# Hand-written unrolling of the inner loops, and a narrower wait in the linear attention, in a four-stage transformer kernel

## The reference

```python
# block 1: linear attention and a mixture of four dense experts (cut)
q_phi, k_phi = elu(q) + 1.0, elu(k) + 1.0           # 16 heads of 8
kv_prefix = cumsum(k_phi[..., :, None] * v[..., None, :], axis=1)
k_prefix = cumsum(k_phi, axis=1)
attn = einsum('bthd,bthdm->bthm', q_phi, kv_prefix) / (sum(q_phi * k_prefix, -1) + 1e-06)
x = x + sigmoid(delta @ w_gate.T + b_gate) * (attn @ w_o.T)
...
# block 2: mixture of 16 experts, fp4 weights; block 3: (x Wq^T) x^T x
# block 4: DEPTH = 6 layers, each
x = attn_layer(shift_tokens(x), Wqkv[i], ...) + x   # 16 heads of 64, windows of 32
x = ffn_layer(shift_tokens(x), ...) + x             # gated GELU, 341 hidden units
```

## Time and profile before

| what | value |
|---|---|
| median of 3 runs | 5524.06 us (5520.37 to 5528.53) |
| the profiled execution | 5523.19 us |
| its span, first to last instruction | 5521.5 us |
| mean granted TensorE clock | 0.937 of full speed |
| busy share of the span | TensorE 89%, VectorE 73%, ScalarE 69%, GpSimd 44% |
| linear attention, steps | about 102 us to 431 us of the span |
| windowed transformer, layers | about 1450 us to 5483 us |

### The profile page before, as it was taken

How to read it: one execution, slowest core, us unless ns; L and a number is a source line. 1 busy time by engine, 2 the same in 40 slices (tenths; PEclk the granted TensorE clock), 3 DMA queues, 4 the chain that set the end, 5 groups by cost and what they waited for, 6 DMA issues and landing times. The chain is left out here.

```text
span 5521.5 us, 148534 instructions
## 1 busy us (share of the span) xinstructions
PE 4891.5 (89%) x42260; PEld 4068.6 (74%) x42260; DVE 4018.0 (73%) x11109; ACT 3813.8 (69%) x12437; POOL 2456.8 (44%) x3763
## 2 busy tenths in 40 slices
PE   5996959996199997999889998899989999799994
PEld 3555948985178886888778887788867888688873
DVE  4554766777678876888768887788867888688875
ACT  1333423342189995999869997799968999599982
POOL 0000000000456664666636665566636666366661
PEclk7996969998599999999999999999999999999997
DMA  0001200000111111111111111111111111111111
GB/s 21 0 0 35 57 1 1 0 0 1 45 29 25 25 37 39 24 24 25 51 25 25 25 25 47 29 25 25 25 45 29 25 25 26 53 23 25 25 49 29
DMA packets 103071, 144.74 MB, mean 26 GB/s; under 512 B 65245, under 2 KB 72690, under 8 KB 102386
## 3 DMA queue, kind: packets, MB, share of 16 engines
q1 hardware_dynamic: 93410, 107.27, 8.6%
q0 software_dynamic: 9232, 33.12, 1.9%
HBM read 49.13 MB, written 2.10 MB: 9 GB/s over the span
## 5 line engine op out<-in xcount | busy, mean ns | idle before, releaser
L2036 ACT ACTIVATE d_probs<-d_S_ps,d_neg_max 128x96 f32<-128x96 f32 x3072 | 1003.0, 342 | 35.3 <-issue 23.0
L1637 POOL TENSOR_TENSOR d_qk<-d_qk,d_sin_terms 128x512 f32<-128x512 f32 x768 | 961.2, 1273 | 29.9 <-DVE d_sin_terms L2223 29.9
L1812 PEld LDWEIGHTS d_S_ps<-d_kT,d_q_blocks 128*128 128x128 f32 x6144 | 791.0, 192 | 2.3
L1812 PE MATMUL d_S_ps<-d_kT,d_q_blocks 128*128 128x96 f32 x6144 | 790.1, 272 | 0.0
L2223 DVE TENSOR_TENSOR d_qk<-d_A_ps,d_tables 128x512 f32<-128x512 f32 x768 | 527.8, 687 | 232.8 <-ACT d_squares L1992 166.0
L2036 ACT ACTIVATION_READ_ACCUMULATOR d_probs<-d_S_ps,d_neg_max 128x1 f32 x3072 | 638.6, 208 | 0.0
L1769 PE MATMUL d_A_ps<-d_wqkv_hi,d_xT_hi 128*128 128x512 f32 x1152 | 558.6, 485 | 19.3 <-DVE d_sin_terms L2223 14.6
L1992 ACT ACTIVATE d_squares<-d_A_ps 128x512 f32<-128x512 f32 x768 | 462.4, 602 | 125.9 <-PE d_A_ps L1771 125.4
L2223 DVE TENSOR_TENSOR d_sin_terms<-d_A_ps,d_tables 128x512 f32<-128x512 f32 x768 | 523.0, 681 | 0.0
L2044 ACT ACTIVATE d_probsT<-d_PT_ps 96x512 f32<-96x512 f32 (+1 forms) x768 | 460.3, 599 | 80.5 <-PE d_PT_ps L1822 80.3
L1776 PE MATMUL d_T_ps<-d_ident,d_qk 128*128 128x128 f32 x3072 | 483.2, 280 | 33.1 <-POOL d_qk L1674 29.1
(11 more groups left out here) (406 smaller groups left out, 10801.4 us busy)
## 6 DMA issues: line engine op xcount, KB each, us to landing
d_v_early<-d_v SPq DMA_DIRECT2D x192, 256.0 KB, 2.9
d_v_early<-d_v SPq DMA_DIRECT2D x192, 128.0 KB, 2.3
d_tables<-L_ffn_rotary POOLq DMA_DIRECT2D x7, 2048.0 KB, 8.4
d_qk<-L_ffn_Wqkv POOLq DMA_DIRECT2D x21, 512.0 KB, 3.9
d_xs<-d_xb SPq DMA_DIRECT2D x56, 127.0 KB
d_xs<-d_xb SPq DMA_DIRECT2D x96, 63.5 KB
ax_fp_blocks<-L_ffn_blocks_gu SPq DMA_DIRECT2D x16, 256.0 KB, 3.9
ax_fp_scales<-L_ffn_scales_gu SPq DMA_DIRECT2D x64, 64.0 KB, 3.4
```

Of the source, the lines that this page charges most:

```text
L1637: nc.gpsimd.tensor_tensor(c4[:, :, s, :], c4[:, :, s, :], s4[:, :, 1 - s, :], ALU.add).then_inc(rotated, 1)
L1812: last = nc.tensor.matmul(S[g % 2][:, n * SEEN:(n + 1) * SEEN], qx[:, p, half, :], kT[b][jj][:, p, HALF * half:HALF * half + SEEN], start= ...
L2036: nc.scalar.activation(pr[:, g, n, seen_columns(g)], S[g % 2][:, n * SEEN:(n + 1) * SEEN], ACT.Exp, bias=nmax[:, g, n:n + 1], accum_out=de ...
```

## The change

All inner hardware loops of the linear attention and of the windowed transformer become Python loops, which write the code out; the loops over the six layers stay. One wait changes.

```diff
@@ linear attention, GpSimd
-                    with pool.Fori(0, J) as j:
+                    for j in range(J):
@@ products
                         pe.wait_ge(qx_ready, u * 4 + 4)
-                        pe.wait_ge(kx_ready, u * 4 + 4)
+                        pe.wait_ge(kx_ready, u * 4 + (g + 1))
                         pe.wait_ge(masked, u * 4 + (g + 1))
@@ linear attention, TensorE; the same on ScalarE, and on VectorE with (u + 1) // 2
-                    with pe.Fori(0, STEPS // 2 - 1) as i:
-                        for par in range(2):
-                            step(i * 2 + (1 + par), 1 - par)
+                    for u in range(1, STEPS - 1):
+                        step(u, u % 2)
@@ tiles_of_layer, all engines but SyncE
-            with engine.Fori(0, J // 2 - 1) as i:
-                for jj in range(2):
-                    for b in range(B):
-                        tile(i * 2 + jj, jj, b, pair=i)
-            tile(J - 2, 0, 0)
-            tile(J - 2, 0, 1)
+            for j in range(J - 1):
+                for b in range(B):
+                    tile(j, j % 2, b, pair=j // 2)
@@ SyncE, tiles
-                    with sp.Fori(0, J // 2 - 1) as i:
-                        for jj in range(2):
-                            shift_tile(i * 2 + jj, jj)
-                    shift_tile(J - 2, 0)
+                    for j in range(J - 1):
+                        shift_tile(j, j % 2)
@@ SyncE, groups
-                        if g is not last_group:
+                        if g < GROUPS - 1:
...
-                    with sp.Fori(0, GROUPS - 1) as g:
+                    for g in range(GROUPS):
                         shift_group(g)
-                    shift_group(last_group)
@@ feed-forward groups, TensorE; the same on ScalarE, and on VectorE from group 2
-                    with pe.Fori(0, GROUPS // 2 - 1) as i:
-                        for gp in range(2):
-                            g = i * 2 + gp
-                            hidden_units(g + 1, 1 - gp)
-                            outputs(g, gp)
+                    for g in range(GROUPS - 2):
+                        hidden_units(g + 1, (g + 1) % 2)
+                        outputs(g, g % 2)
```

More of the change, by code:

```diff
@@ L859, in _ @@
                     step(0, 0, first=True)
-                    with act.Fori(0, STEPS // 2 - 1) as i:
-                        for par in range(2):
-                            step(i * 2 + (1 + par), 1 - par)
+                    for u in range(1, STEPS - 1):
+                        step(u, u % 2)
                     step(STEPS - 1, 1, last=True)
@@ L982, in _ @@
                     step(0, 0, 0, first=True)
-                    with v.Fori(0, STEPS // 2 - 1) as i:
-                        for par in range(2):
-                            step(i * 2 + (1 + par), i + 1, 1 - par)
+                    for u in range(1, STEPS - 1):
+                        step(u, (u + 1) // 2, u % 2)
                     step(STEPS - 1, J - 1, 1, last=True)
@@ L1583, in shift_tile @@
                         shift_rows(j, 1)
-                    with sp.Fori(0, J // 2 - 1) as i:
-                        for jj in range(2):
-                            shift_tile(i * 2 + jj, jj)
-                    shift_tile(J - 2, 0)
+                    for j in range(J - 1):
+                        shift_tile(j, j % 2)
                     shift_tile(J - 1, 1, last=True)
-                    last_group = GROUPS - 1
                     def shift_group(g):
@@ L2193, in group @@
                             split_group(m0 + (g + 1))
-                    with act.Fori(0, GROUPS // 2 - 1) as i2:
-                        for gp in range(2):
-                            group(i2 * 2 + gp, gp)
+                    for g in range(GROUPS - 2):
+                        group(g, g % 2)
                     group(GROUPS - 2, 0, more=1)
@@ L2440, in _ @@
                     v.sem_inc(waits_met)
-                    with v.Fori(1, GROUPS // 2 - 1) as i2:
-                        for gp in range(2):
-                            group(i2 * 2 + gp, gp)
+                    for g in range(2, GROUPS - 2):
+                        group(g, g % 2)
                     group(GROUPS - 2, 0, more=1)
```

## The result

| | before | after |
|---|---|---|
| median (range) in the runs taken side by side | 5526.3 us (5520.4 to 5532.5) | 5435.8 us (5429.9 to 5439.3) |
| span of the profiled execution | 5521.5 us | 5433.2 us |

The ratio is 0.983, with a 95% interval of 0.9815 to 0.9845.

The account below looks back on a forecast made before the run. TensorE, busy 89% of the span, was taken as the bound; 27.9 + 10 + 22 + 5 + 2 = 67 us off 5523.2 gave 5456, rounded to 5458 us. Own range 5444 to 5470, 8-in-10 range 5440 to 5476.

Parts of the forecast that it names:

- The wait on k: Linear attention: first product waits only for the first k copy, saving 0.90 us in 31 steps, 27.9 us (26.4 to 29.1).
- With the same 0.23 us hand-over: Linear attention: last k copy to product takes 0.23 us, taken as unchanged; TensorE's idle before the product was 0.94 us.
- The clock: Linear attention: 7 falls of TensorE's clock vanish with the idle before the first product, 7 x 1.42 = 10 us.
- The rival that it still falls: Linear attention: clock falls stay, 5467 us, or come every third step, 5471 us; chance 0.2.
- its other bound: Linear attention: clock falls come more often, every third step, 10 falls, -4 us.
- Back-edges: Attention-tile loop: 0.61 us saved at each of 36 taken back-edges, 22 us (bounds 5 and 23).
- the 0.61 us is ScalarE's: Tile-loop back-edges: extra 0.61 us comes from ScalarE's "issue" stall before its first exponentials; TensorE then waits for v's copy.
- Register work: Attention tiles: written-out tiles 28 and 29 show 0.03 us less a tile, 168 tiles, 5 us (bounds 0 and 17).
- The rest: Feed-forward loop edges and register work on entering the loops: together 2 us, bounds 0 and 6.
- Fetching: Written-out tiles: rival that 180 more instruction packets are fetched and uncovered fetches bound the kernel, 5667 us; chance 0.03.
- the sentence on the first pass: Tile loop: each layer's first pass is already fetched this way, yet its tiles take 17.27 to 17.29 us.
- SyncE's layer branch: Layer loop: SyncE's longer body may make its branch stall, 3.5 us at most; covered, so costed at nothing.

Follow-up runs that it names:

- experiment 1: Kernel before with only the wait on k narrowed to the product's own group, all loops kept: 5485.7 us, ratio 0.9928.
- experiment 2: Changed kernel with the old wait put back, so that every product waits for all four k groups: 5484.0 us, ratio 0.9923.
- experiment 6: Changed kernel with ScalarE's loop over attention tiles alone put back: 5464.5 us, ratio 0.9885.
- experiment 11: Changed kernel with the loops over attention tiles put back on VectorE and GpSimd: 5461.6 us, ratio 0.987.
- experiment 5: Changed kernel with TensorE's loop over attention tiles alone put back: 5457.5 us, ratio 0.9877.
- experiment 9: Changed kernel with two waits ahead of k's transposes getting the same values by a longer formula: 5480.2 us, ratio 0.9905.
- experiment 10: Changed kernel with two such waits, on counts long met, put ahead of the last chunk of the projection: 5434.8 us, ratio 0.9827.
- experiment 7: Changed kernel with the loops over feed-forward groups put back on TensorE, ScalarE and VectorE: 5434.3 us, ratio 0.9836.
- experiment 3: Kernel before with only the linear attention as changed (written out, narrower wait), windowed transformer with its loops: 5485.1 us, ratio 0.9926.
- experiment 8: Changed kernel with the loop over the six layers written out too, on all five engines: 5409.6 us, ratio 0.9798.
- experiment 12: Changed kernel with no hardware loop left (layers, expert stages and both short stages ahead of the attention written out): 5408.6 us, ratio 0.9785.
- experiment 4: Kernel before with only the windowed transformer written out, linear attention as before: 5479.3 us, ratio 0.9912.

## Why the prediction was wrong, and where it was right

**The wait on k.** The mechanism is shown (experiments 1 and 2). The size was off: 1.05 us a step, not 0.90. The step that failed is "With the same 0.23 us hand-over", capped at "the whole 0.94": the hand-over is 0.10 us, and the idle is counted from the modelled end of the update, which lies 0.07 us behind the start of the product in the changed kernel. 29 steady steps x 0.15 = 4.4 us of the 6.7 by which this stage beat its forecast. Another 1.6 is an eighth fall of the clock, in the second step (11.49 us; granted clock 0.51 from 114.2 to 117.6 us), which the forecast's seven leave out and which is gone too; the rest lies in the first step and the last ones. My reason for a shorter hand-over, a register instruction less, is right, but there are two ways to lose it: constants do it (experiment 2, 0.10 us with the old wait), and so does the narrower wait by itself, whose value is that of the next wait (experiment 1, 0.1 us with the loops in place).

**The clock.** Right, and shown from both sides. The rival that it still falls was wrong for the change. Experiment 2 met its other bound, a fall every third step, with shorter steps and the idle still there.

**Back-edges.** 22 us were forecast. The edges gained 0.70 us, of which 0.12 belong to every tile: 36 x 0.58 = 21 us. ScalarE's branch as the cause is shown (experiment 6), but "the 0.61 us is ScalarE's" was incomplete. VectorE had a stall of its own under it, worth 0.38 us (experiment 11), and by that reckoning, which was not run, the term came true only because the change wrote out both.

**Register work.** This is the step that put the time outside the range: "Tiles 28 and 29 ... show what a tile costs after the change ... That is 0.03 us a tile". They don't: their average mixes a tile that still has two register instructions ahead of k's load (28: 17.31 us from start to start, 0.31 between the loads) with one that has a single one (29: 17.16 us, 0.17). Tile 29 alone was representative, and I had it as the upper bound (0.1 us, 17 us). Measured: 0.11 to 0.12 us a tile, 19.8 us by experiment 5 instead of 5. What was missing was the question where the instruction stands. Experiments 9 and 10 answer it: with the same number of them in a tile, but more of them right ahead of a load that nothing hides, a tile takes 0.18 us more; two behind three queued products cost nothing that shows.

**The rest.** 2 us forecast, 6.4 in the traces (1.6, 1.2 and 3.6). The feed-forward loops are not shown to be its cause (experiment 7); these stretches differ by as much between profiles whose code there is the same (transitions of 605.9 us in experiment 5, 611.0 in the changed kernel).

**Fetching** never became a bound, as the sentence on the first pass argued: 242 more packets on queue 8 (180 were reckoned), and the steady tiles are shorter. SyncE's layer branch, costed at nothing, took 54 ns at most.

**The sum.** By the traces the kernel gained 21.3 us more than the 67 forecast: 6.7 in the linear attention, 11 in the tiles (15 more by register work, less 1 at the edges and less some 3 for the uneven tiles below), 4.4 in the rest, and -0.6 at the first product. The medians add 2 to that.

## What to carry to other kernels

When an engine's register instruction is to be priced, find the load or product behind it: here it cost about its full time where that load wasn't queued ahead, and nothing that shows under queued work. Two waits in a row that want the same value need one register instruction less between them. When a stall at a loop's edge is put down to one engine, look for a second engine's smaller stall at the same edge before removing the first; ask of each loop alone what it would leave. And a written-out tile is a sample of the kernel to come only if it has the same instructions at the place that matters; compare two such tiles with each other before averaging them.

## What was not expected of the hardware

- **Idle moves the clock's rhythm.** With the same idle of 0.8 to 0.95 us at one place of each step, steps of 9.89 us had a fall of the clock in every fourth, steps of 9.73 us in every third (experiment 2). The added falls took back the whole gain of the shorter steps.
- **The clock's return at the start of the linear attention is a matter of the execution.** In programs whose code is the same there, one profile has TensorE at half clock from 106 to 120 us and another at full clock; steps afterwards are equal, and the stage differs by 7 us (291.6 against 284.5). Experiments 5, 6, 7, 10 and 11 have the long form, the changed kernel and experiments 3, 8, 9 and 12 the short one. The kernel before rose at 107.3 us, so the two traces laid side by side in the table are both of the early kind; against one of the other kind the gain of this stage would have read 37.4 us, near the forecast's 38 by luck. The stretch in experiment 7 and in the changed kernel:

```profile
106.00:120.00 14.00, 14.00 (x83) 8.70 (x83) 4.25 (x12) 2.98 (x12) 0.65 (x2) 0.50 0.00 1
```
```profile
106.00:120.00 14.00, 14.00 (x136) 8.96 (x135) 8.58 (x23) 4.17 (x17) 1.33 (x4) 1.00 0.01 2
```

- **Straight code isn't quite even.** In the changed kernel the same tiles of every layer are longer: the seventh interval 17.25 us, the sixteenth 17.33, the twenty-fifth 17.31 (means over the layers). In the seventh and the sixteenth GpSimd's copy of x (L1708) comes 0.26 to 0.28 us late, in the twenty-fifth ScalarE's exponentials (L2023) 0.16. The bump at the twenty-fifth is gone with ScalarE's loop back (17.15, experiment 6), the one at the seventh with VectorE's and GpSimd's (17.17, experiment 11); the sixteenth is itself an edge in both, so they can't tell. In experiment 4, whose tile code is the same behind a shorter program, the first two are 17.17 and 17.24. That looks like the fetch of the next piece of code, but no run shows it. It costs 2 to 3 us in all.
- **The gap between two loads has to be read with the one before it.** The spacing of the x and k loads alone doesn't order the steady tiles: 0.125 us in experiment 8, with no register instruction anywhere, went with tiles of 17.17 us, and 0.167 in the changed kernel with 17.15. Counted from the last load of the scores (L1801 here) to the k load, medians over all such tiles are 0.225 us (experiment 10, tiles of 17.09), 0.319 (changed, 17.15), 0.331 (experiment 8, 17.17), 0.424 (before, 17.27) and 0.501 (experiment 9, 17.33). In experiment 8 the wait ahead of x's transpose has become a sequencer instruction of its own, so that the x load comes 0.205 us behind the scores' instead of 0.152, and what k's load gained there is lost again:

```profile
L1742 PEldq EVENT_SEMAPHORE  x186: 51/51/51, 1425.8 to 5219.1; - x186
```

The rule holds to 0.02 us only: experiments 2, 4 and 11 have 0.320 to 0.326 with tiles of 17.17, which stays open.
